# A transformer block on Trainium2: one merged token loop instead of two, and weight-quantizing DMAs on GpSimd's queue

## What is computed

```python
xn = layernorm(x)
x = x + attn(xn) + ffn(xn)

def attn(x):                       # linear attention and an MLP
    xn = rmsnorm(x, scale1)
    q, k, v = qkv_w @ xn           # 16 heads of 64
    q, k = exp(-0.5*q*q), exp(-0.5*k*k)
    out = q @ (k^T v) / (q . k.sum(2) + 1e-6)
    x = x + gamma * (proj_w @ out + proj_b)
    xn2 = rmsnorm(x, scale2)
    hdd = gelu(conv1_w @ xn2 + conv1_b)        # 2048 wide
    return x + gamma * (conv2_w @ hdd + conv2_b)

def ffn(x):                        # every linear: both operands to FP4
    h = silu(w_gate(x)) * w_up(x)  # 2816 wide, in blocks of 16, and back
    return w_down(h)
```

## Time and profile before

| | us |
|---|---|
| median of the 2 runs (4167.77 and 4168.09) | 4167.93 |
| the profiled execution | 4193.16 |
| its span on the slowest core (6) | 4191.6 |
| spans of the other cores | 4132.9 to 4179.0 |
| setup and stage A, to the start of the projection weights' loads | 1346 |
| stage B | to 1810 |
| stage B2 | to 2853 |
| F1 and F2 | to the end |

### The profile page before, as it was taken

One profiled execution on the slowest core, in us unless ns is written; L12 is line 12 of the kernel. 1 busy time (PEld: TensorE's weight loads), 2 busy tenths in 40 slices (PEclk: granted clock), 3 DMA queues, 4 the chain that ended last, 5 costly groups with the idle time before them and its releaser, 6 DMA issues.

```text
span 4191.6 us, 28650 instructions; the slowest of 8 cores (4132.9 to 4191.6 us)
## 1 busy us (share of the span) xinstructions
PE 1676.5 (40%) x7488; PEld 727.7 (17%) x7488; DVE 2256.8 (54%) x3809; ACT 785.4 (19%) x1179; POOL 643.2 (15%) x381
## 2 busy tenths in 40 slices
PE   0544444446776223310332333261623432341179
PEld 0212211123333101100111111020211111120033
DVE  2777777777752255521655555540476667667201
ACT  0322222324443010000111111110212211221000
POOL 0111111111100010000211111100333323332000
PEclk9877777778898556655665666575766666665578
DMA  4111111112121412124111111117000000000652
GB/s 151 61 53 53 53 58 61 53 53 76 56 79 33 110 53 69 61 98 127 48 56 37 56 48 52 41 53 153 12 14 7 14 14 14 8 14 14 121 127 86
DMA packets 225800, 245.71 MB, mean 59 GB/s; under 512 B 173284, under 2 KB 173284, under 8 KB 224614
## 3 DMA queue, kind: packets, MB, share of 16 engines
q1 hardware_dynamic: 214086, 211.37, 17.6%
q10 hardware_dynamic: 11520, 32.51, 2.0%
q0 software_dynamic: 32, 0.00, 0.0%
HBM read 135.85 MB, written 66.58 MB: 48 GB/s over the span
## 4 chain that ended last, share of the span: by engine, by line
DVE 42%; PE 22%; DMA 12%; issue 10%; ACT 5%; SPq 4%; POOL 3%; DVEq 1%; ACTq 0%; POOLq 0%
DVE q_m L376 4%; DVE q_lt L373 4%; PE KV L920 4%; DMA xb<-x_all 4%; DMA wldB<-conv_wT 3%; DVE q_amax L330 2%; DVE q_g L409 2%; DVE q_m L406 2%; DVE q_m L400 2%; DVE q_m L394 2%; DVE q_m L388 2%; DVE q_m L382 2%; PE PA L995 2%; DVE q_m L403 2%; DVE q_m L391 2%
## 5 line engine op out<-in xcount | busy, mean ns | idle before, releaser
L355 POOL TENSOR_TENSOR q_ss<-q_sgn,q_hs 128x1024 f32<-128x1024 f32 (+1 forms) x140 | 256.0, 1829 | 2677.8 <-DVE q_hs L346 2210.1
L995 PE MATMUL PA<-wgT,xqTall 128*128 128x512 bf16 x384 | 117.9, 459 | 621.5 <-ACT hsila L1009 536.6
L373 DVE TENSOR_SCALAR q_lt<-q_a 128x1024 bf16<-128x1024 f32 (+1 forms) x140 | 166.5, 1189 | 322.2 <-POOL q_a L360 322.2
L360 POOL TENSOR_TENSOR q_a<-q_a,q_inv 128x1024 f32<-128x1024 f32 (+1 forms) x140 | 279.7, 1998 | 0.0
L565 PE MATMUL PA<-wTs,xTb 128*128 128x512 bf16 x256 | 132.2, 516 | 276.5 <-ACT xTb L561 276.5
L565 PE MATMUL PA<-wTs,xTa 128*128 128x512 bf16 x256 | 126.8, 495 | 289.5 <-ACT xTa L561 289.5
L376 DVE TENSOR_SCALAR q_m<-q_a 128x1024 bf16<-128x1024 f32 (+1 forms) x140 | 193.9, 1385 | 0.0
L995 PEld LDWEIGHTS PA<-wgT,xqTall 128*128 128x128 bf16 x384 | 41.6, 111 | 684.3 <-issue 660.6
L326 ACT ACTIVATE q_a<-wqld 128x1024 f32<-128x1024 f32 x76 | 71.7, 944 | 438.0 <-DVE xqB L412 255.1
L1073 PE MATMUL PA<-wdT,hqTall 128*128 128x512 bf16 x176 | 79.3, 451 | 173.1 <-DMA hqTall<-hqspill 173.1
L565 PE MATMUL PB<-wTs,xTb 128*128 128x512 bf16 x256 | 130.1, 508 | 0.0
(11 more groups left out here) (234 smaller groups left out, 4477.0 us busy)
## 6 DMA issues: line engine op xcount, KB each, us to landing
xb<-x_all SPq DMA_DIRECT2D x64, 512.0 KB, 3.8
wldB<-conv_wT SPq DMA_DIRECT2D x32, 512.0 KB, 3.6
wld<-qkv_wT SPq DMA_DIRECT2D x8, 1536.0 KB, 6.8
wqld<-w_gate SPq DMA_DIRECT2D x22, 512.0 KB, 4.5
wqld<-w_up SPq DMA_DIRECT2D x22, 512.0 KB, 5.2
wqld<-w_down SPq DMA_DIRECT2D x16, 704.0 KB, 5.0
hqspill<-hq ACTq DMA_DIRECT2D x16, 704.0 KB, 3.1
wgq<-wqout SPq DMA_DIRECT2D x22, 256.0 KB, 2.2
```

The lines of the kernel that those rows point to most:

```text
L355: oprw(p, 'gpsimd', lambda g, NB=NB, W=W, sgn=sgn, hs=hs, ssb=ssb: g.tensor_tensor(ssb.ap[:, 0:W].rearrange("p (a b) -> p a b", b=QB), sgn ...
L360: oprw(p, 'gpsimd', lambda g, NB=NB, W=W, inv=inv, qa=qa: g.tensor_tensor(qa.ap[:, 0:W].rearrange("p (a b) -> p a b", b=QB), qa.ap[:, 0:W] ...
L373: oprw(p, 'vector', lambda g, W=W, q_a=q_a: g.tensor_scalar(q_lt.ap[:, 0:W], q_a.ap[:, 0:W], 0.25, None, ALU.is_gt), reads=[q_a], writes=[ ...
L995: oprw(p, 'tensor', lambda T, kc=kc, occ=occ, w=w, pg=pg, t=t: T.matmul(pg.ap[:, 0:w], xqTallC[kc].ap[:, kc * S_core + t * 128:kc * S_core ...
```

## The change

Three things are changed.

1. The two DMAs of a weight job (lines 485 and 499) are issued by POOL's queue instead of SP's.
2. The stages B and B2 become one loop over the 16 own tiles. All three weights are loaded ahead of it, in pieces of 128 x 512 (80 of them) through one buffer of 128 x 512. Neither `oacc` nor `xn2` goes through DRAM; `xn2` is transposed on PE and copied by ACT (838, 842). x is loaded and normalized once. `hdd` is transposed and multiplied in two rounds of 8 blocks through one bf16 buffer `x2T1`, which the transposed `xn2` uses too; `outz1` serves for three things; x and `oacc` share three buffers.
3. All 16 weight jobs left over after stage A are in this loop, one per tile.

```diff
-        dmarw(p, 'sync', lambda E, ...: E.dma_start(     # load of a weight job
+        dmarw(p, 'gpsimd', lambda E, ...: E.dma_start(
...
-        dmarw(p, 'sync', lambda E, ...: E.dma_start(     # store of a weight job
+        dmarw(p, 'gpsimd', lambda E, ...: E.dma_start(
...
-    wldB = SB('wldB', [128, HID], F32, stack=esB)
+    wldB = SB('wldB', [128, 512], F32, stack=esB)
     for kc in range(8):
+        for hf in range(2):      # projT: 16 pieces
...
+    for kc in range(8):
+        for hf in range(4):      # conv1: 32 pieces
...
+    for kc in range(16):
+        for hf in range(2):      # conv2: 32 pieces
...
+    def stageS1(t):              # = stageBb(t), and for x:
         oprw(p, 'vector', lambda v, ...: v.tensor_scalar(
             xn.ap[:], x.ap[:], ...))
+        emit_quant_pre(xn, 0, C, QSET0 if t % 2 == 0 else QSET1)
...
+    def stageS2(t):              # transpose xn2, conv1, Gelu
+        prA, prB = pairof(t + 1)
+        C1B = (prA, prB, KV1, KV2)
...
+    def stageS3(t):              # conv2 in two rounds, + oacc, then
+        emit_quant_main(xqB21, 0, C, QSET0 if t % 2 == 0 else QSET1)
...
+    stageBld(0)
     for t in range(T_own):
+        if t >= 2:
+            stageS3(t - 2)
         if t + 1 < T_own:
+            stageBld(t + 1)
         if wj_i < len(wjobs):
             emit_wjob(wj_i, QSET0 if t % 2 == 0 else QSET1)
             wj_i += 1
+        stageS1(t)
+        if t >= 1:
+            stageS2(t - 1)
+    if T_own >= 2:
+        stageS3(T_own - 2)
+    stageS2(T_own - 1)
+    stageS3(T_own - 1)
```

More of the change, by code:

```diff
@@ L703, in stageBa @@
             writes=[x])
[L705 to L714, removed]
+    def stageS1(t):
+        x = oaT[t % 3]
+        xn = xnB1
+        x1 = x1B
+        oacc = oaT[t % 3]
+        xn2 = xn2P[t % 2]
+        outz = outz1
+        ozT = outz1
+        mv = mvP[t % 2]
         oprw(p, 'vector', lambda v, x=x, xn=xn, t=t: v.tensor_scalar(
@@ L802, in stageBb @@
             reads=[x1, mv], writes=[xn2])
[L803 to L841, removed]
-    x2Tallh = esB2.enter_context(nc.sbuf_tensor('x2Tall', [128, 8 * S_core], BF16))
-    x2TallC = [Buf(x2Tallh, f'x2Tall{j}') for j in range(8)]
@@ L874, in stageB2q @@
-    def stageB2q(t):
-        xq = xqB2P[t % 2]
-        emit_quant_main(xq, 0, C, QSET0 if t % 2 == 0 else QSET1)
-        dmarw(p, 'scalar', lambda E, t=t, xq=xq: E.dma_start(
-            d_xqspill[t * 128:(t + 1) * 128, :], xq.ap[:]), 'xqs', reads=[xq])
[L880 to L883, removed]
+    def stageS2(t):
+        xn2 = xn2P[t % 2]
+        hdd = hddP[t % 2]
+        for kc in range(8):
+            oprw(p, 'tensor', lambda T, kc=kc, xn2=xn2: T.transpose(
+                TR.ap[:, kc * 128:(kc + 1) * 128],
+                xn2.ap[:, kc * 128:(kc + 1) * 128], ident.ap[:]),
+                reads=[xn2, ident], writes=[TR])
+        oprw(p, 'scalar', lambda sc: sc.copy(x2T1.ap[:], TR.ap[:]),
+             reads=[TR], writes=[x2T1])
+        prA, prB = pairof(t + 1)
+        C1B = (prA, prB, KV1, KV2)
@@ L913, in stageB2c @@
                     reads=[hdd, ident], writes=[TR])
[L914 to L924 removed]
+            oprw(p, 'scalar', lambda sc: sc.copy(hdT1.ap[:], TR.ap[:]),
+                 reads=[TR], writes=[hdT1])
+            for hh in range(2):
+                pbk = prA if hh == 0 else prB
+                for kc in range(8):
+                    kk = rnd * 8 + kc
+                    oprw(p, 'tensor', lambda T, kc=kc, kk=kk, hh=hh, pbk=pbk: T.matmul(
+                        pbk.ap[:], hdT1.ap[:, kc * 128:(kc + 1) * 128],
+                        c2TgC[kk].ap[:, kk * C + hh * 512: kk * C + (hh + 1) * 512],
+                        start=(kk == 0), stop=False),
+                        reads=[hdT1, c2TgC[kk]], writes=[pbk])
+        for hh in range(2):
+            pbk = prA if hh == 0 else prB
             oprw(p, 'tensor', lambda T, hh=hh, pbk=pbk: T.matmul(
@@ L957, in build_nc @@
     p.barrier()
-    esB2.close()
+    esB.close()
     esW.close()
```

146 lines of the change are left out of this document (63 added, 83 removed).

## The result

| | us |
|---|---|
| changed kernel, median of 11 runs (4237.9 to 4312.2) | 4246.2 |
| kernel before, median of 10 runs on the same chip (4167.4 to 4254.3) | 4171.3 |
| ratio | 1.019, 95% interval 1.0145 to 1.0237 |
| span of the profiled execution, slowest core (1) | 4236.3 |

The forecast was 4231 with a range of 4140 to 4325. The change costs 1.9%, and the interval runs from 1.5% to 2.4%. In some executions of any of these kernels the cores of one die, or of both, show a lower granted clock than the others and take some per cent longer, and the ratios compare only executions without that.

A forecast was written before the change was run, and what follows sets the result against it. The prediction took waits on DVE's in-order list as the bound, no engine being full. Stage A -93 and the merged stretch +156 (weights +101 included) gave +63 on 4168, so 4231 us, range 4140 to 4325.

The forecast's parts named there:

- Stage A, -93: Stage A: the wait for x goes, a shorter one for the job's load follows; -93 us, from -120 to +5.
- the 0.9 taken twice for a POOL DMA: Stage A: POOL is held 0.9 us each by the job's store and by the load's issue behind it.
- z: Stage A: the end of line 412 in a tile; the job's data were expected 6.15 us after it, 7.87 before.
- The pairs after tile 34: Stage A from tile 34, a job every second tile: 3.7 us gained per pair, 10 pairs, 37 us (5 to 45).
- Weights, +101: Loading the loop's weights: 80 half loads in turn through one buffer take 299 us for 198, +101 (+29 to +157).
- The merged loop, +55: The merged stretch without its weight loading: 55 us longer, as conv2's chain is bare in DVE's list; tile 83.8 us.
- W: Merged loop: DVE's wait for conv2 at the add in each tile, 24.4 us forecast, nothing of it covered.
- Rival 4: Merged loop's chain slower still: PE slow in conv2 too, or POOL's products holding up line 746; 4290 to 4385, chance 0.08.
- The table load, +18: Merged loop: ACT's table load before each Ln is bare on DVE's path, 14 tiles x 1.3 = +18 us.
- Rival 1: Stage A's wait goes altogether, 170 us for 93, because the job's load lands in time; 4154 us, chance 0.14.
- Rival 2: Stage A: POOL's DMAs are slow beside a busy DVE, deciding from 1.8 us per issue; 4324 us, chance 0.12.
- Rival 3: Loop's weights: half a load costs as much as a whole one, 80 x 0.7 more; 4287 us, chance 0.10.

The follow-up runs named there:

- experiment 6: The changed kernel with the next weight job's load issued on POOL ahead of the store in stage A: 4154.7 us, ratio 0.996 to the kernel before.
- experiment 1: The kernel before with only the two DMAs of a weight job moved to POOL's queue, stages unmerged: 4009.4 us, ratio 0.963.
- Experiment 3: The changed kernel with the loop's weights loaded in 40 whole pieces through one buffer instead of 80 halves: 4165.5 us, ratio 1.0004 to the kernel before.

## Why the forecast held, point by point

**Stage A, -93; measured -88.4.** The mechanism is right: x is early, and the job's load behind the store is late next (experiment 6 takes that wait away and gains it in full). The sizes were off in three places that cancel on this core, which is luck. Per tile the gain was 2.35 us, not 1.7: 21 jobs from the first store to the 22nd take 529.9 us before (124.2 to 654.1) and 480.5 after (138.4 to 618.9). The term that was mis-sized most is the 0.9 taken twice for a POOL DMA. It lasts 0.53 to 0.60, and a landing counts from the start of an issue, so only the store's 0.60 stands ahead of the load's 4.6 us. Against that POOL starts the store 0.63 us after line 412, not 0.15, and the landing was 4.6 and not the least, 4.2. So line 330 starts at z + 5.9 and not z + 6.15; the rest of the tile, from line 330 to the end of line 412, is shorter by some 0.3 us more, and why is not shown. That is 78 for 56 over 33 tiles.

The pairs after tile 34 gave 25 for 37, by difference. The waits show where the rest went: line 515's 50 us for x are gone there, but lines 537 and 543 wait 85 us for ACT's line 527 where it was 64. And the first store comes 14 us later on this core, which the forecast did not have at all. On the mean of the eight cores it is 10.6 us later, and 8 in the kernels of experiments 1 and 3. The timeline of core 1 shows three parts. The second job's load waits on POOL behind line 360 (issued at 116.71, where SP did it at 105.60), and line 330 waits 3.9 for it. Lines 403 and 406 then fall beside POOL's two products and take 2.42 and 2.23 us for 0.69 each, 3.3 more. The other 6.4 are in the setup, 4.5 of them DVE's wait for `proj_b` (19.9 instead of 15.4 us); why was not tried.

**Weights, +101; measured +110 in the table, +103 by the forecast's own count.** The mechanism and the size are right. The new steps came to 302.8 for 299, and the stretch before was 199.6 for 198; a half load lands in 2.8 us (proj) and 3.0 (conv), and 2.9 was taken. Experiment 3 confirms it from the other side.

**The merged loop, +55; measured +58 in the table, +65 by the forecast's own count.** W was forecast at 24.4 and is 23.8. The tile was 83.8 plus 1.3 for the table load; it is 85.6 (line 894 from 1680.5 to 2878.7 in 14 tiles). The missing 1.1 (0.6 less of W, 0.5 more in all) is mostly a thing that the forecast did not have: line 772, a product of 128 x 16 values, took 0.175 us in stage B, where it stood alone (line 740 there), and takes 1.04 here (median; once 0.69, once 3.15).

```profile
L772 DVE TENSOR_SCALAR den<-den x16: 691/1044/3153, 1591.2 to 2835.4; 128x16 f32<-128x16 f32 x16
```

```profile
2064.03 1.93 POOL L355 TENSOR_TENSOR q_ss<-q_sgn,q_hs 128x1024 f32<-128x1024 f32 x1 [2.60 <-DVE q_hs L346]
2064.94 1.05 DVE L772 TENSOR_SCALAR den<-den 128x16 f32<-128x16 f32 x1
2065.92 1.92 POOL L360 TENSOR_TENSOR q_a<-q_a,q_inv 128x1024 f32<-128x1024 f32 x1
```

It ends at 2065.99, 0.03 after POOL's product (2065.96), and in all 16 tiles it ends 0.03 to 0.04 us after one of POOL's products. The quantization of x, moved ahead of the attention part, lets POOL start just there. Rival 4 had POOL hold up line 746 and had the right kind of cause at the wrong place: line 746 is not stretched, line 772 is, by 0.87 us a tile.

**The table load, +18.** As an instruction on DVE's path it is as priced: line 830's wait falls from 1.98 to 0.70 without it, 1.28. As a term of the time it is smaller: taking it away gains 7 us of 18, so this term was right as a price and too large as a gain to be had back. The Trainium skill (ScalarE: Activation LUTs, "What ACT_TABLE_LOAD costs") adds a drain of 1380 ns; here the Ln starts 0.02 us after the load (1997.34) and the wait differs by 1.28, so the trace shows no drain on this path.

**Rival 1 (A's wait goes altogether, 4154)** did not happen by the change, and for the reason given: the load landed 4.6 us after an issue that has to follow the store. Experiment 6 made it happen.

**Rival 2 (POOL's DMAs slow beside DVE, 4324)** fell, by its own test: 0.53 to 0.72 us where it needed more than 1.8. The Trainium skill (SBUF: State Buffer, "SBUF: two separate sides") has the port that GpSimd and VectorE share as a lock, held for a whole instruction by the one that starts first, where VectorE's operation is in a two-port mode or reads two SBUF inputs. The rows agree with that (line 772 ends with POOL's product, POOL's load 0.12 us after line 376), and they show why it costs so little here: DVE's instructions last 0.6 to 0.7 us when POOL doesn't hold them, so a DMA waits for the rest of one of them. The page's figure for a held-up DMA, about 3.1 us against 0.62 alone, is not reached in any run here.

**Rival 3 (half a load costs a whole one)** fell: 2.8 to 3.0 against 3.6.

What the forecast did not ask is what each part is worth alone. Its time was right to 15 us (4231 for 4246), but that time joins a gain of 156 (experiment 1) with a loss of some 230.

## What to carry to other kernels

When stages are merged, lay the in-order list of the busiest engine out over one tile and look at its last instruction: if the next one needs the end of a chain that starts only there, the chain is bare, and moving work between the two instructions is worth the whole wait (356 us here, with nothing added). A load loop through one buffer pays the landing time per piece, and half a piece lands hardly sooner than a whole one (2.8 to 3.0 us for 3.6): 80 halves took 299 us, 40 whole pieces 202, and the same 40 over four buffers 67. Rotate over tiles that the next stage holds anyway. A store that waits for its data blocks every load behind it on the same queue; put the load first, or on another queue, and look into the other stages for the same pair before counting the gain.
